# Layer normalization statistics taken batch by batch in the stage ahead, in a 4-layer decoder on one core

## The reference

```python
def _layernorm(x, axis=-1, eps=1e-05):
    m = jnp.mean(x, axis=axis, keepdims=True)
    v = jnp.var(x, axis=axis, keepdims=True)
    return (x - m) / jnp.sqrt(v + eps)

x = x + _L0_attn_ref(_layernorm(x), ...)                # l0a: causal attention, 16 heads
x = x + _L0_xattn_ref(ctx, ctx, _layernorm(x), ...)     # l0x: attention to the context
x = x + _L0_ffn_ref(_layernorm(x), ...)                 # l0m: experts
x = x + _L1_attn_ref(_layernorm(x), ...)                # l1a: linear attention
x = x + _L1_xattn_ref(_layernorm(x), ctx, ...)          # l1c: co-attention
x = x + _L1_ffn_ref(_layernorm(x), ...)                 # l1m: experts
x = x + _L2_attn_ref(_layernorm(x), ...)                # l2a: softmax over queries
x = x + _L2_xattn_ref(_layernorm(x), ctx, mask, ...)    # l2x: attention to the context
x = x + _L2_ffn_ref(_layernorm(x), ...)                 # l2h, l2f: experts of attention, then a small MLP
x = x + _L3_attn_ref(_layernorm(x), ...)                # l3a: softmax over the batch
x = x + _L3_xattn_ref(_layernorm(x), ctx, ctx, ...)     # l3x: attention to the context, 16 heads
x = x + _L3_ffn_ref(_layernorm(x), ...)                 # l3m: experts
```

## Time and profile before

| | us |
|---|---|
| median of 3 runs | 2515.73 (2515.11, 2515.73, 2526.72) |
| profiled execution, own time | 2529.61 |
| its span | 2527.8 |
| busy PE / PEld | 2150.0 (85%) / 1505.0 (60%) |
| busy DVE | 1750.9 (69%) |
| busy ACT | 1222.3 (48%) |
| busy POOL | 1196.7 (47%) |
| mean granted TensorE clock | 0.903 |

### The profile page before, as it was taken

One profiled execution on the slowest core, in us unless ns is written; L12 is line 12 of the kernel. 1 busy time (PEld: TensorE's weight loads), 2 busy tenths in 40 slices (PEclk: granted clock), 3 DMA queues, 4 the chain that ended last, 5 costly groups with the idle time before them and its releaser, 6 DMA issues. The chain is left out here.

```text
span 2527.8 us, 38017 instructions
## 1 busy us (share of the span) xinstructions
PE 2150.0 (85%) x12870; PEld 1505.0 (60%) x12870; DVE 1750.9 (69%) x3675; ACT 1222.3 (48%) x2513; POOL 1196.7 (47%) x1368
## 2 busy tenths in 40 slices
PE   6999759664799987576999999999999976869698
PEld 3666548454588865363666666666666635548454
DVE  5777658545588874656777777778776654479498
ACT  6887535222466654132444444544444443435365
POOL 5331028001499960005776667667666600014298
PEclk8999869766899999667999999999999988879699
DMA  1000024000466630012234443333433331000273
GB/s 47 2 3 2 7 55 109 7 6 20 100 156 156 151 70 19 1 54 50 65 81 98 88 96 89 88 95 86 94 81 84 74 68 39 1 1 1 49 172 96
DMA packets 62984, 161.92 MB, mean 64 GB/s; under 512 B 7563, under 2 KB 18571, under 8 KB 55000
## 3 DMA queue, kind: packets, MB, share of 16 engines
q1 hardware_dynamic: 62792, 159.50, 27.1%
HBM read 156.46 MB, written 3.01 MB: 63 GB/s over the span
## 5 line engine op out<-in xcount | busy, mean ns | idle before, releaser
L2192 PE MATMUL bank<-l2h_og,l2h_wo 128*128 128x512 f32 x512 | 260.5, 593 | 2.5 <-DVE LNT L2452 1.6
L2302 ACT ACTIVATE l2h_pr<-twin,l2h_nmx 128x512 f32<-128x512 f32 x256 | 176.0, 688 | 152.9 <-PE bank L2181 105.6
L1079 POOL TENSOR_TENSOR l1m_hid_lo<-l1m_hid,l1m_hid_hi 128x512 fp32r<-128x512 f32 x136 | 218.9, 1629 | 62.7 <-ACT l1m_hid_hi L1058 62.1
L2294 ACT ACTIVATE l2h_prT<-bank 128x512 f32<-128x512 f32 x256 | 151.7, 593 | 195.4 <-PE bank L2181 195.4
L2455 DVE TENSOR_REDUCE l2h_nmx<-twin 128x2 f32<-128x1024 f32 x128 | 156.1, 1219 | 92.3 <-PE twin L2170 92.2
L2526 POOL TENSOR_TENSOR l2h_vs<-l2h_vg 128x256 f32<-128x256 f32 x256 | 192.7, 753 | 20.6 <-DVE l2h_vg L2428 20.6
L2428 DVE TENSOR_TENSOR l2h_vg<-bank,l2h_gv 128x512 f32<-128x512 f32 x256 | 174.8, 683 | 34.5 <-POOL l2h_vs L2526 21.7
L2440 DVE TENSOR_TENSOR l2h_og<-bank,l2h_gt 128x512 f32<-128x512 f32 x256 | 173.0, 679 | 7.1 <-DMA l2h_gt<-l2m_gate_rows 4.4
L1923 POOL TENSOR_TENSOR l3x_pr<-l3x_pr,l3x_rs 128x1232 f32<-128x1232 f32 x16 | 35.9, 2249 | 282.9 <-DVE l3x_rs L1944 282.9
L2521 POOL TENSOR_TENSOR l2h_plain<-l2h_plain,l2h_rotated 128x512 f32<-128x512 f32 x64 | 82.4, 1288 | 173.7 <-DVE l2h_rotated L2421 173.7
L2181 PE MATMUL bank<-ident,l2h_pr 128*128 128x128 f32 x1024 | 161.0, 280 | 0.0
(11 more groups left out here) (642 smaller groups left out, 6028.9 us busy)
## 6 DMA issues: line engine op xcount, KB each, us to landing
l2h_gt<-l2m_gate_rows SPq DMA_DIRECT2D x128, 512.0 KB, 7.1
l1m_c<-l1m_weights SPq DMA_DIRECT2D x64, 512.0 KB, 6.4
l3m_c<-l3m_weights SPq DMA_DIRECT2D x32, 512.0 KB, 6.4
l0m_c<-l0m_weights SPq DMA_DIRECT2D x16, 512.0 KB, 6.8
l1m_w<-in_l1m_pairs SPq DMA_DIRECT2D x32, 192.0 KB, 6.4
l2h_fresh<-in_l2m_wqkv SPq DMA_DIRECT2D x8, 768.0 KB, 4.8
l2h_wo<-in_l2m_wo SPq DMA_DIRECT2D x8, 512.0 KB, 3.9
l0m_w<-in_l0m_pairs SPq DMA_DIRECT2D x8, 192.0 KB, 4.9
```

Source lines behind the costliest of these rows:

```text
L1079: nc.gpsimd.tensor_tensor(hid_lo[:, at, :], hid[:, (n + PRE) % 4, :], hid_hi[:, at, :], ALU.subtract)\
L2192: nc.tensor.matmul(ybank[:, :], wo[s][:, e, :], og[:, e % 4, :], start=(e == 0), stop=(e == E - 1))\
L2294: nc.scalar.activation(prT[:, j // 2 % 2, h, :, j % 2 * P:(j % 2 + 1) * P], tbank[:, :].rearrange("p (c q) -> p c q", c=TPB), ACT.Copy).th ...
L2302: nc.scalar.activation(pr[:, h, :], sbank[:, h, :], ACT.Exp, bias=nmx[:, k % 2, h:h + 1], accum_out=rs[:, g % 2, t, h:h + 1]).then_inc(exp ...
```

## The change

The statistics of a batch are taken by DVE right behind the addition that completes the batch, in the stage ahead of the normalization, by `token_stats`; `T.ln_known` lists the tiles done, and `layernorm` takes only those that are not. It applies to 13 of the 14 normalizations: the first (input X) takes all its statistics as before, and the last stage (l3m) has none behind it. `roots_next` puts one root of a column of zeros at the end of ACT's stream of a stage (in `expert_ffn` in front of its four last copies, in l2h in front of the copies to LNX), so that the compiler's table load comes there. In l2a and l3a the statistics of the batch (or tile) before come after the next one's values; elsewhere directly behind the addition. The one addition of LNX to X is cut into four, by batch, each with its statistics.

```diff
+def token_stats(nc, T, link, src, tiles):
+    for t in tiles:
+        out = nc.vector.bn_stats(T.ln_stats[:, t, :], src[:, t, :])
+    link(out)
+    for t in tiles:
+        out = nc.vector.bn_aggr(T.ln_mv[:, t, :], T.ln_stats[:, t, :])
+    T.ln_known += tiles
+    return out
+
+def batch_tiles(b):
+    return list(range(b * TPB, (b + 1) * TPB))
+
+def roots_next(nc, T):
+    nc.scalar.activation(T.rooted[:, :], T.zeros[:, 0:1], ACT.Sqrt)
...
@@ layernorm, vector
-            for t in range(NT):
-                out = nc.vector.bn_stats(T.ln_stats[:, t, :], src[:, t, :])
-            link(out)
-            for t in range(NT):
-                out = nc.vector.bn_aggr(T.ln_mv[:, t, :], T.ln_stats[:, t, :])
-            link(out)
+            unknown = [t for t in range(NT) if t not in T.ln_known]
+            if unknown:
+                link(token_stats(nc, T, link, src, unknown))
+            T.ln_known = []
...
@@ l0_attention, vector, behind the addition L292 (l1a behind L1370 and l1c behind L1529 alike)
+                        dve.wait_ge(added, b + 1)
+                        token_stats(nc, T, link, T.X[:, :, :], batch_tiles(b))
@@ l0_attention, scalar, at the end (context_attention, l1a, l1c, l2a, l3a, l3x, l2f alike)
+                roots_next(nc, T)
...
@@ context_attention, vector, behind L791 (l3x behind L1949 alike)
+                        if tile % TPB == TPB - 1:
+                            dve.wait_ge(added, tile + 1)
+                            token_stats(nc, T, link, T.X[:, :, :], batch_tiles(tile // TPB))
...
@@ expert_ffn, scalar, in front of L1068 (followed is False in l3m)
                 steps(step)
+                if followed:
+                    roots_next(nc, T)
                 for c in range(B):
@@ expert_ffn, vector
-                    nc.vector.tensor_tensor(x, x, T.bank[4 + c][:, :].rearrange("p (t d) -> p t d", t=TPB), ALU.add)
+                    add = nc.vector.tensor_tensor(x, x, T.bank[4 + c][:, :].rearrange("p (t d) -> p t d", t=TPB), ALU.add)
+                    if followed:
+                        link(add)
+                        token_stats(nc, T, link, T.X[:, :, :], batch_tiles(c))
...
@@ l2_attention, vector (l3_attention alike, with tile t of every batch)
+                def measure(b):
+                    dve.wait_ge(added, b + 1)
+                    token_stats(nc, T, link, T.X[:, :, :], batch_tiles(b))
...
                                             spread(rs[:, b % 2, :], D), ALU.mult).then_inc(v_scaled, 1)
+                    if b:
+                        measure(b - 1)
                 add_output(B - 1)
+                measure(B - 1)
...
@@ l2h, vector, at the end
                     dve.wait_ge(added, TURNS * GROUPS)
+                    link = chain(T, dve)
+                    for b in range(B):
+                        dve.wait_ge(src_copied, b + 1)
+                        token_stats(nc, T, link, T.LNX[:, :, :], batch_tiles(b))
@@ l2f, vector, behind the addition of a batch to LNX
+                        dve.wait_ge(added, c + 1)
+                        token_stats(nc, T, link, T.LNX[:, :, :], batch_tiles(c))
@@ the block behind the second normalization of LNX
-                nc.vector.tensor_tensor(T.X[:, :, :], T.X[:, :, :], T.LNX[:, :, :], ALU.add)
+                link = chain(T, dve)
+                for b in range(B):
+                    ts = slice(b * TPB, (b + 1) * TPB)
+                    link(nc.vector.tensor_tensor(T.X[:, ts, :], T.X[:, ts, :], T.LNX[:, ts, :], ALU.add))
+                    token_stats(nc, T, link, T.X[:, :, :], batch_tiles(b))
```

More of the change, by code:

```diff
@@ L808, in expert_ffn @@
 def expert_ffn(nc, T, A, name, E, K, route, NSH=1, half_weights=False, add_input=False,
-               counted=False):
+               counted=False, followed=True):
     I = 64
@@ L1815, in add_output, with measure @@
                         .then_inc(added, 1)
+                def measure(t):
+                    dve.wait_ge(added, t + 1)
+                    token_stats(nc, T, link, T.X[:, :, :], [b * TPB + t for b in range(B)])
                 nc.vector.memset(eps[:, :], EPS).then_inc(eps_ready, 1)
@@ L1837, in _ @@
                     nc.vector.tensor_tensor(last_block, last_block, tiled(tril[:, 1, :], B), ALU.add).then_inc(normal, 1)
+                    if t:
+                        measure(t - 1)
                 add_output(TPB - 1)
+                measure(TPB - 1)
 def l3_context(nc, T, A, F):
@@ L1949, in _ @@
                         nc.vector.tensor_tensor(x, x, obank[j % 2][:, 0:D], ALU.add).then_inc(added, 1)
+                        if j % TPB == TPB - 1:
+                            dve.wait_ge(added, j + 1)
+                            token_stats(nc, T, link, T.X[:, :, :], batch_tiles(j // TPB))
 def l3_attentions(nc, T, A):
@@ L2619, in build @@
     T.dve_steps = T.ln_calls = T.ln_affine_calls = 0
-    T.used = []
+    T.used, T.ln_known = [], []
     with ExitStack() as ctx:
@@ L2632, in build @@
         T.rev = sb("rev", [P, 64])
+        T.rooted = sb("rooted", [P, 1])
         T.ln_stats = sb("ln_stats", [P, NT, 6])
```

3 lines of the change are left out of this document (2 added, 1 removed).

## The result

Ten runs of each on one chip: 2507.69 us (2501.15 to 2512.45) against 2524.77 (2513.0 to 2527.18) before. The ratio is 0.9949, 95% interval [0.9933, 0.9966]: about 13 us faster, 8.5 to 17. (The medians lie 17.1 apart and the means 13.6: the ten times of the kernel before form two groups, four at 2513 to 2516 and six at 2524 to 2527, and the median falls into the upper one.) The profiled execution has a span of 2505.9 us.

The account below looks back on a forecast made before the run. No engine is full throughout; each normalization's 4.43 us of DVE statistics lies on the path. Savings 28.3 + 0.8 less 2.4, 11.0 and 0.5 give 15.2 us, from 2515.73 to 2500.5 us; range 2490 to 2515.

Parts of the forecast that it names:

- nine tails: Behind nine stages, only the last statistics follow the last addition: path loses 4.43, gains 1.29, saving 28.3 us in all.
- lumps, three: Behind l0m, l1m and l2f's final addition, additions and statistics alternate on DVE: 0.7, 0.7 and 0.9 us slower, 2.4 together.
- l0a: The next step's mask follows the addition at once, so three insertions of 1.29 are uncovered: 3.9 us, bounds 0 and 4.5.
- l1a: DVE's waits for `twin`, about 0.9 each, partly cover three insertions of 1.29: 1.1 us longer.
- l3x: First insertion fits TensorE's slack, the second costs about 0.3, tile 11 falls into the drain: 0.3 us, bounds 0 and 2.6.
- load of l2x: Counted among the other loads, all except l2h's gate weights, said to land before they are wanted: no cost.
- Rival 1: TensorE's clock is granted more, as its idle gap at normalizations shrinks from 7.45 to 4.3 us: 8.4 us, 2492; chance 13%.
- Rival 2: Table load still stands at the normalization's start, 0.9 us exposed 11 times: gain only 5 us, 2510; chance 12%.
- Rival 3: DVE stalls in l0a, l0x, l1a, l2x lower TensorE's clock, 1.29 + 1.6 us per insertion: 8.9 slower, 2525; chance 15%.
- Rival 4: Interior insertions half hidden by work queued on TensorE and ACT: 5 us in place of 11, 2494.5; chance 12%.
- My test: Prediction is wrong if clock shares in the windows at normalizations differ from now, or stages together lengthen over 20 us.
- The other test: l0a, l0x and l2x, measured from first to last matmul, should be longer by 3.9, 3.1 and 2.6 us.

Follow-up runs that it names:

- e1: Kernel before plus the first three groups' statistics taken a second time in the stages, normalizations left whole, no root of zeros: ratio 1.0057 to the kernel before, +14.4 us.
- e2: Kernel before, but every normalization except the first takes only its last four tiles' statistics, nothing inserted in stages: ratio 0.9843 to the kernel before, −39.6 us.
- e3: Changed kernel without the root of zeros at the end of the stages: ratio 0.9968 to the kernel before, −8.1 us.
- e4: Changed kernel with statistics behind l0m, l1m and before l3a back in the normalization, l2f's final addition one instruction again: ratio 0.9938 to the kernel before, −15.6 us.
- e5: e4 with each statistics group of the first three batches taken three times in l1c, l2a, l2f and l3a: ratio 0.9971 to the kernel before.
- e6: e4 with insertions moved into DVE's waits in l0a and l2x, and last four tiles each behind its addition in l0x, l2x, l3x: ratio 0.9879, −30.5 us.
- e7: Kernel before with only the root of zeros added at the end of the stages' ACT streams: ratio 1.0014 to the kernel before, +3.5 us.
- e9: e4 with three extra bn_stats in front of l2f's final addition, so l3a starts about 1.0 us later: ratio 0.9939 to the kernel before, −15.4 us.
- e11: e4 with nine extra bn_stats in front of l2f's final addition, 2.9 us: ratio 0.9952 to the kernel before, −12.1 us.
- e10: e4 with six extra bn_stats in front of l2f's final addition, 1.9 us: ratio 0.9942 to the kernel before, −14.6 us.

## Why the prediction was right

The median lies inside the range of 2490 to 2515, and the interval of the gain, 12.9 us [8.5, 17], holds the 15.2 forecast. The gain was hit better than the time: 2507.69 is 7.2 over the 2500.5 forecast and outside the 2496 to 2506 that the forecast gave itself. The step behind that is the base. The 15.2 were taken from 2515.73, the median of three runs of which two lay in the lower group; ten runs gave 2524.77. That the time still fell into the range is owed to the range's width. The mechanism and most terms were right. Step by step, with lengths at the same clock:

| term | forecast | measured |
|---|---|---|
| nine tails | −28.3 | −28.2 |
| lumps, three | +2.4 | +2.6 |
| behind l2h | −0.8 | −1.0 |
| l0a | +3.9 | +3.75 at the full clock |
| l0x | +3.1 | +3.2 |
| l2x | +2.6 | +2.45 |
| l1a | +1.1 | +0.3 to 0.4 |
| l1c, l2a, l2f, l3a | 0 | +0.2 |
| l3x | +0.3 | +0.6 |
| load of l2h | +0.5 | +0.65 |
| load of l2x | 0 | +1.3 in this execution |
| sum | −15.2 | −15.4; −14.1 with l2x's load |

(l0a: the three distances of the table in e1 and e2's section; l0x: from first tile to the stage's end, 16.9 against 13.7; load: TensorE idle for 1.68 us in place of 1.03.) The full price in l0a is one whole 1.29 between two masks; DVE in the changed kernel:

```profile
164.74 0.69 DVE L311 TENSOR_TENSOR X<-X,bank 128x512 f32<-128x512 f32 x1 [0.60 <-PE bank L497]
165.46 0.87 DVE L61 BATCH_NORM_STATS2 ln_stats<-X 128x6 f32<-128x128 f32 x4
166.36 0.38 DVE L64 BATCH_NORM_AGGREGATE ln_mv<-ln_stats 128x2 f32<-128x6 f32 x4
166.66 0.39 DVE L261 CUSTOM_DVE_ANT_0 l0a_sc<-l0a_rel,bank 128x256 f32<-128x256 f32 x1
```

The terms of the sum agree with whole runs as well, which they were not fitted to, though the intervals are 8 to 19 us wide. From the same terms (with the leftover waits where they are): e1 +12 (measured 14.4, interval 9.6 to 18.9), e2 −40 (−39.6), e3 −4 (−8.1, −13.1 to −3.0), e4 −18 (−15.6, −21.4 to −9.6), e5 −8 (−7.3, −12.1 to −2.8), e6 −24 (−30.5, −39.8 to −20.9), e7 +2 (3.5, −2.0 to 8.8), e9 to e11 −17, −16 and −15 (−15.4, −14.6, −12.1).

- **l1a was mis-sized**: I subtracted DVE's wait for `twin` (0.9) from 1.29 and charged the rest. The distances grew by 0.3 to 0.4 in all, in place of 1.1. My guess, which no run tests, is that TensorE had other work in front of the product that needs DVE; then an idle time of DVE is only a lower bound of the cover.
- **The loads were priced one short.** "The other loads land before they are wanted" failed for l2x in the changed kernel's trace and in e5's: DVE waited 1.58 and 1.37 us for the mask bits in place of 0.30. Seven other kernels with the shortened path got them in time.
- **l3x** was right in kind and small: +0.6 in place of +0.3. Additions of tiles 3 to 6 in the changed kernel:

```profile
2278.82 0.23 DVE L2006 TENSOR_TENSOR X<-X,bank 128x128 f32<-128x128 f32 x1
...
2285.24 0.23 DVE L2006 TENSOR_TENSOR X<-X,bank 128x128 f32<-128x128 f32 x1
2290.35 0.23 DVE L2006 TENSOR_TENSOR X<-X,bank 128x128 f32<-128x128 f32 x1
2295.46 0.23 DVE L2006 TENSOR_TENSOR X<-X,bank 128x128 f32<-128x128 f32 x1
```

  Between tile 3 and 4 lie 6.42 us, 1.02 more than the 5.40 of a step before. Then DVE runs without a pause at 5.11 per step and wins back 0.29 in each. It has three such steps before the next insertion and two behind it: 0.15 of the first and 0.45 of the second stay.
- **Rival 1 (clock)** did not come as told. The transposes of the normalizations ran at the low level still: from L110 to the last copy it took 6.35 us in seven of the twelve without gain and 6.18 to 6.31 in the others, as before the change (6.19 to 6.36). Behind the stages the granted clock over the transposes was 0.50 to 0.68, before 0.50 to 0.54. The Trainium skill, "TensorE: Matmul & The Clock Gate", section "HAM oscillation — how this bites in real kernels", says that the clock falls in an idle gap of TensorE of a few us, so that the work behind it starts at the low clock; the trace agrees for the 4.34 us gap. The clock's part was real but elsewhere: l2h moved by −4.1 us, l1a by −3.1 and l2a by +2.3, where the insertions cost 0.4 at most. The trace of before had shown the two levels, and my 1.8 and 3 us for it had the right size per stage and one sign too few.
- **Rival 2 (load at the normalization)** was excluded by the trace after, and e3 shows its price. The drain of the Trainium skill ("ScalarE: Activation LUTs", "What ACT_TABLE_LOAD costs", about 2.66 us with it) does not appear: in e3's rows the root begins 0.02 us behind the load's 1.28, and in the changed kernel the load at 275.70 begins 0.02 behind the copy before it and the root of zeros 0.01 behind the load.
- **Rival 3 (the stages give it back)** fell: an insertion costs 1.3 where it is exposed, not 2.2. Its clock fall was seen once in each of two traces (e1, e9: l0a's third distance), but traces without insertions have one in l0a as well. **Rival 4** too: in l0a, l0x and l2x nothing was absorbed.
- **My test was too coarse.** I had written that clock shares other than before would make the prediction wrong. They were other in half of the stages and the sum held, because their differences came with both signs. The other test failed for the same reason: l0a, l0x and l2x were to be 3.9, 3.1 and 2.6 longer and are 0.5, 1.2 and 5.6 longer as whole stages, while between their additions the insertions cost what was forecast. In the two profiles the spans differ by 21.9 us; 6 to 8 of them are such differences and not the change.

## What to carry to other kernels

Price an edit between two instants that it touches, not by stage or span: here most terms held to 0.3 us while whole stages moved by 2 to 4 for another reason. Say at which clock an interval was measured, and count those that you leave out. Work put behind an instruction costs its full length where the engine's next instruction follows at once and feeds TensorE, and nothing where the engine waits for longer than that; the idle column says which, and moving the same work by a few steps of the loop took back half to all of it. Where additions already come one after another on the engine that would do the statistics, taking them apart only adds waits.

## What the runs showed of the hardware

- One stage with one list of instructions lasted 99.9, 103.8, 105.65 and 108.3 us (l3a, e11, e4, e10, e9), with a granted clock of 0.915, 0.885, 0.835 and 0.808 over the stage. The same for l2a: 48.7, 50.3 and 52.6 us at 1.00, 0.97 and 0.92.
- At the start of the kernel the same four matmuls took 3.75 us in some executions and 1.96 in others, with a recorded clock of 1.00 in both.
- The load of `l2x_keep_bits`, issued at the same place, took 3.0 to 3.5 us to land in eleven of thirteen traces and 4.4 and 4.6 in two.
- Executions of one binary lie in two groups 12 us apart, which differ in the mean granted clock (0.910 and 0.905). Three runs would not have told the change's 13 us from that.
- An engine that waits once more at the end of a stage, with nothing behind the wait, puts off the next block by 0.22 us (4.97 against 4.75, nine times).
